# GpSimd multiplies by gamma ahead of the next power, and the tests of the group slots are written another way

## The reference

```python
h_nr  = gelu(x @ w1_nr  + b1_nr)  @ w2_nr  + b2_nr      # condition 0 ("NR")
h_tsr = gelu(x @ w1_tsr + b1_tsr) @ w2_tsr + b2_tsr     # condition 1 ("TSR")
h     = gelu(x @ w1_sr  + b1_sr)                        # condition 2 ("SR"), 512 wide
h_sr  = gelu(h @ w2_sr  + b2_sr)  @ w3_sr  + b3_sr
y = x + (the one that the condition picks, or zeros)
out = (y - mean(y)) * rsqrt(var(y) + 1e-5) * gamma + beta
```

## Time and profile before

| | us |
|---|---|
| median of 3 runs | 112.78 |
| the runs | 111.09, 112.78, 112.89 |
| the profiled execution | 111.2 |
| its span | 109.5 |
| busy: PE, DVE, POOL, ACT | 86.0, 77.6, 68.3, 64.3 |
| first product of the first group | 14.5 |
| TensorE's last instruction ends | 94.7 |
| last scatter issued | 104.87 |

### The profile page before, as it was taken

One profiled execution on the slowest core, in us unless ns is written; L12 is line 12 of the kernel. 1 busy time (PEld: TensorE's weight loads), 2 busy tenths in 40 slices (PEclk: granted clock), 3 DMA queues, 4 the chain that ended last, 5 costly groups with the idle time before them and its releaser, 6 DMA issues.

```text
span 109.5 us, 1829 instructions
## 1 busy us (share of the span) xinstructions
PE 86.0 (79%) x503; PEld 74.9 (68%) x503; DVE 77.6 (71%) x193; ACT 64.3 (59%) x104; POOL 68.3 (62%) x78
## 2 busy tenths in 40 slices
PE   0269969999999999999999999999999976600000
PEld 0157568868889888798998989989899866500000
DVE  5579084762555572839989899899998889699800
ACT  0575229995986045895977959779595870330000
POOL 6427910019777630000796988979879798999850
PEclk9999999999999999999999999999999999995555
DMA  0794788100498991000000404022040130103153
GB/s 2 264 311 142 234 258 298 34 0 3 94 343 205 419 407 73 0 6 0 0 6 22 175 3 174 6 87 105 6 192 6 73 130 6 54 0 154 40 216 144
DMA packets 5459, 12.84 MB, mean 117 GB/s; under 512 B 688, under 2 KB 2752, under 8 KB 5440
## 3 DMA queue, kind: packets, MB, share of 16 engines
q0 software_dynamic: 2880, 9.96, 25.5%
q1 hardware_dynamic: 2540, 2.63, 7.3%
q10 hardware_dynamic: 20, 0.01, 0.0%
HBM read 8.40 MB, written 4.72 MB: 120 GB/s over the span
## 4 chain that ended last, share of the span: by engine, by line
PE 67%; POOL 13%; DVE 4%; DMA 4%; issue 4%; POOLq 2%; ACT 1%; ACTq 1%
PE ps_a L732 8%; PE ps_a L734 8%; PE ps_a L733 7%; PE ps_x L713 7%; PE ps_f L786 6%; PE ps_f L788 6%; PE ps_f L787 6%; POOL xs L346 4%; POOL xs L341 4%; PE ps_f L814 4%; DMA bias_rows<-L_cond_b_sr_dram 4%; PE ps_f L777 3%; POOL rstd L331 3%; PE ps_b L807 2%; PE ps_b L808 2%
## 5 line engine op out<-in xcount | busy, mean ns | idle before, releaser
L331 POOL TENSOR_TENSOR rstd<-hvar,half 128x4 f32<-128x4 f32 x9 | 9.4, 1040 | 15.6 <-DVE hvar L598 15.5
L788 PE MATMUL ps_f<-wf_hi,f_hi 128*128 x64 | 17.9, 280 | 0.0
L786 PE MATMUL ps_f<-wf_hi,f_lo 128*128 x64 | 17.9, 280 | 0.0
L787 PE MATMUL ps_f<-wf_lo,f_hi 128*128 x64 | 17.9, 280 | 0.0
L732 PE MATMUL ps_a<-x_hi,w_lo 128*128 128x512 f32 x40 | 16.5, 413 | 1.1 <-DVE x_lo L643 1.1
L409 ACT ACTIVATE f_hi<-ps_a,bias_cols 128x512 fp32r<-128x512 f32 x16 | 11.0, 688 | 9.6 <-PE ps_a L808 4.7
L734 PE MATMUL ps_a<-x_hi,w_hi 128*128 128x512 f32 x40 | 15.7, 393 | 0.0
L733 PE MATMUL ps_a<-x_lo,w_hi 128*128 128x512 f32 x40 | 15.6, 390 | 0.0
L299 POOL DMA_INDIRECT xs<-x_dram,load_idx x11 | 11.1, 1012 | 6.5 <-DVE load_idx L538 3.6
L413 ACT ACTIVATE xs<-xs,shift,rstd 128x256 f32<-128x256 f32 x23 | 12.1, 593 | 4.3 <-POOL shift L335 4.3
L346 POOL TENSOR_TENSOR xs<-xs,beta_b 128x768 f32<-128x768 f32 (+1 forms) x8 | 14.1, 1762 | 0.5
(11 more groups left out here) (124 smaller groups left out, 191.3 us busy)
## 6 DMA issues: line engine op xcount, KB each, us to landing
w_raw<-L_cond_w_sr_dram SPq DMA_DIRECT2D x2, 512.0 KB, 4.6
wf_raw<-L_cond_w_sr_dram SPq DMA_DIRECT2D x1, 256.0 KB, 5.3
w_raw<-L_cond_w_tsr_dram SPq DMA_DIRECT2D x1, 256.0 KB, 6.5
w_raw<-L_cond_w_nr_dram SPq DMA_DIRECT2D x1, 256.0 KB, 6.8
wf_raw<-L_cond_w_tsr_dram SPq DMA_DIRECT2D x1, 256.0 KB, 6.9
wf_raw<-L_cond_w_nr_dram SPq DMA_DIRECT2D x1, 256.0 KB, 7.1
xs<-x_dram,load_idx POOLq DMA_INDIRECT x11, 6.5
out_dram<-xs,store_idx POOLq DMA_INDIRECT x9, 3.4
```

Source lines behind the costliest of these rows:

```text
L331: nc.gpsimd.tensor_tensor(rstd[:, g, :], hvar[:, g, :], half[:, :], ALU.pow).then_inc(rstd_step, 1)
L786: nc.tensor.matmul(dst, fl[:, kt, toks], w_hi, start=False, stop=False)
L787: nc.tensor.matmul(dst, fh[:, kt, toks], w_lo, start=False, stop=False)
L788: mm = nc.tensor.matmul(dst, fh[:, kt, toks], w_hi, start=False, stop=last)
```

## The change

On GpSimd, times_gamma of group g-1 moves from behind root and shifted of g to in front of them (function pool_group); beta and scatter stay behind. In all engines but SyncE, each_step takes the place of the loops with by_place: the first eight slots are not tested, from slot 8 on an empty slot leads to the finish of the group before it, whose instructions stand directly behind the step that ran. As each route's branch now holds the whole step, TensorE's last layer stands in both. SyncE waits for slots 0 to 6 without tests, then for 10, 9, 8 behind tests, then for 7.

The diff, cut to what matters:

```diff
--- before.py
+++ after.py
@@ -210,31 +210,38 @@
             eng.load(regs, cls_tab[0:1, 0:SLOTS])
             return [eng.snap(r, min_val=0, max_val=EMPTY) for r in regs]
 
-        def by_place(eng, cls, g, normal, second, last):
-
-            def end():
-                if g + 1 < MIN_GROUPS:
-                    second(g)
-                elif g + 1 < SLOTS:
-                    with eng.If(cls[g + 1] < EMPTY):
-                        second(g)
+        def each_step(eng, cls, step, finish):
+
+
+            for s in range(SLOTS + 1):
+                if s < MIN_GROUPS:
+                    step(s)
+                elif s < SLOTS:
+                    with eng.If(cls[s] > NR):
+                        if s == MIN_GROUPS:
+                            finish(s - 1)
+                        else:
+                            with eng.If(cls[s - 1] < EMPTY):
+                                finish(s - 1)
+                            with eng.Else():
+                                pass
                     with eng.Else():
-                        last(g)
+                        step(s)
                 else:
-                    last(g)
-
-            if g + 2 < MIN_GROUPS:
-                normal(g)
-            elif g + 2 < SLOTS:
-                with eng.If(cls[g + 2] < EMPTY):
-                    normal(g)
+                    with eng.If(cls[s - 1] < EMPTY):
+                        finish(s - 1)
+                    with eng.Else():
+                        pass
+
+        def if_next(eng, cls, s, part):
+
+            if s + 1 < MIN_GROUPS:
+                part(s + 1)
+            elif s + 1 < SLOTS:
+                with eng.If(cls[s + 1] < EMPTY):
+                    part(s + 1)
                 with eng.Else():
-                    end()
-            else:
-                end()
-
-        def nothing(g):
-            pass
+                    pass
 
         @block.sync
         def _(sp):
@@ -257,11 +264,14 @@
                 sp.dma_start(W_F[i][0], W_F[i][1]).then_inc(w_in[4 + i], 16)
             sp.wait_ge(tab_done, 1)
             cls = load_classes(sp, "sp_cls")
-            for s in range(SLOTS):
+            for s in range(MIN_GROUPS - 1):
+                sp.wait_ge(stored[s], 16)
+            for s in reversed(range(MIN_GROUPS, SLOTS)):
                 with sp.If(cls[s] < EMPTY):
                     sp.wait_ge(stored[s], 16)
                 with sp.Else():
                     pass
+            sp.wait_ge(stored[MIN_GROUPS - 1], 16)
 
         @block.gpsimd
         def _(pool):
@@ -356,26 +366,27 @@
                     in_=xs[g][:, :, :].rearrange("p t h -> p (t h)"), in_offset=None,
                     bounds_check=last_row, oob_is_err=False).then_inc(stored[g], 16)
 
-            def middle(g):
+            def pool_group(g):
+                if g > 0:
+                    times_gamma(g - 1, POOL_TT)
                 root(g)
                 shifted(g)
                 if g > 0:
-                    times_gamma(g - 1, POOL_TT)
                     plus_beta(g - 1, POOL_TT)
                     scatter(g - 1, False)
 
-            def final(g):
+            def pool_step_of(s):
+                if s > 0:
+                    pool_group(s - 1)
+
+            def pool_finish(g):
                 times_gamma(g - 1, 2)
                 root(g)
                 plus_beta(g - 1, 2)
                 scatter(g - 1, False)
                 scatter(g, True)
 
-            for g in range(SLOTS):
-                with pool.If(cls[g] < EMPTY):
-                    by_place(pool, cls, g, middle, middle, final)
-                with pool.Else():
-                    pass
+            each_step(pool, cls, pool_step_of, pool_finish)
 
         @block.scalar
         def _(act):
@@ -438,50 +449,37 @@
...
+            def act_step(s):
+                f = f_hi[s % 2]
                 if s > 0:
-                    next_x(s)
...
+            each_step(act, cls, act_step, lambda g: normed_second(g - 1))
@@ -646,54 +644,41 @@
...
+            def norm_part(s):
+                if s >= 1:
+                    middle(s - 1)
+                if s == 2:
+                    dve.wait_ge(gamma_done, 1)
+                if s >= 2:
+                    gamma_beta_one(s - 2)
...
+            each_step(dve, cls, dve_step_of, final)
@@ -816,27 +791,24 @@
             pe.wait_ge(bias_done, 1)
             pe.wait_ge(tab_done, 1)
             cls = load_classes(pe, "pe_cls")
-            for s in range(SLOTS + 1):
-                if s < SLOTS:
-                    with pe.If(cls[s] < EMPTY):
-                        if s > 0:
-                            pe.wait_ge(x_lo_done, upto_x(s))
-                            next_x(s)
-                        with pe.If(cls[s] < TSR):
-                            long_first(s)
-                        with pe.Else():
-                            with pe.If(cls[s] < NR):
-                                short_first(TSR, s)
-                            with pe.Else():
-                                short_first(NR, s)
+            def pe_step(s):
                 if s > 0:
-                    with pe.If(cls[s - 1] < EMPTY):
-                        by_place(pe, cls, s - 1, to_f, to_f, to_x)
+                    pe.wait_ge(x_lo_done, upto_x(s))
+                    if_next(pe, cls, s, transpose_x)
+                with pe.If(cls[s] < TSR):
+                    long_first(s)
+                    if s > 0:
+                        last_layer(s - 1, ps_f)
+                    long_second(s)
+                with pe.Else():
+                    with pe.If(cls[s] < NR):
+                        short_first(TSR, s)
                     with pe.Else():
-                        pass
-                if s < SLOTS:
-                    with pe.If(cls[s] < TSR):
-                        long_second(s)
+                        short_first(NR, s)
+                    if s > 0:
+                        last_layer(s - 1, ps_f)
+
+            each_step(pe, cls, pe_step, lambda g: last_layer(g, ps_x))
 
 
 # ---- launch: one core; inputs and outputs as the reference has them ----
```

More of the change, by code:

```diff
@@ new lines, in act_step @@
+            def act_step(s):
+                f = f_hi[s % 2]
+                if s > 0:
+                    if_next(act, cls, s, x_high)
+                with act.If(cls[s] < TSR):
+                    bias_at = act.snap(cls[s].with_bounds(max_val=SR) * 4)
+                    banks = (ps_a[0], ps_a[1], ps_b, ps_a[0])
+                    for m in range(HT):
+                        gelu(banks[m][:, 0, :], h_hi[:, m, :], bias_cols[:, bass.ds(bias_at + m, 1)],
+                             HID * s + m + 1, 1)
+                        if s == 0 and m == 0:
+                            x_high(1)
+                    if s == 0:
+                        other_routes()
+                    if s >= 2:
+                        normed(s - 2)
+                    for m, bank in ((0, ps_a[1]), (1, ps_b)):
+                        gelu(bank[:, 0, :], f[:, m, :], bias_cols[:, 14 + m:15 + m], HID * s + HT + m + 1, 1)
+                with act.Else():
+                    if s == 0:
+                        other_routes()
+                    bias_at = act.snap(cls[s].with_bounds(max_val=NR) * 4)
+                    for m in range(2):
+                        gelu(ps_a[m][:, 0, :], f[:, m, :], bias_cols[:, bass.ds(bias_at + m, 1)],
+                             HID * s + SHORT[m], SHORT_STEP[m])
+                        if s == 0 and m == 0:
+                            x_high(1)
+                    if s >= 2:
+                        normed(s - 2)
@@ L647, in _ @@
             cls = load_classes(dve, "dve_cls")
[L649 to L656, removed]
-                if s > 0:
-                    next_x(s)
[L659 to L690, removed]
-                    with dve.Else():
-                        pass
-                if s < SLOTS:
-                    with dve.If(cls[s] < TSR):
-                        for m, bank in ((0, ps_a[1]), (1, ps_b)):
-                            low(bank[:, 0, :], f[:, m, :], f_l[:, m, :], HID * s + HT + m + 1, 1)
@@ new lines, in norm_part, with dve_step_of @@
+            def norm_part(s):
[3 more added lines that the diff above has]
+                    dve.wait_ge(gamma_done, 1)
+                if s >= 2:
+                    gamma_beta_one(s - 2)
+            def dve_step_of(s):
+                f, f_l = f_hi[s % 2], f_lo[s % 2]
+                if s > 0:
+                    if_next(dve, cls, s, x_low)
+                with dve.If(cls[s] < TSR):
+                    banks = (ps_a[0], ps_a[1], ps_b, ps_a[0])
+                    for m in range(HT):
+                        low(banks[m][:, 0, :], h_hi[:, m, :], h_lo[:, m, :], HID * s + m + 1, 1)
+                        if s == 0 and m == 0:
+                            x_low(1)
+                    if s == 0:
+                        w_low(2)
+                        w_low(3)
+                    norm_part(s)
```

(11 more changed lines are left out.)

54 lines of the change are left out of this document (2 added, 52 removed).

## The result

| | before | changed |
|---|---|---|
| median, us | 112.03 (111.09 to 112.89, 4 runs) | 114.14 (113.35 to 114.41, 4 runs) |
| ratio | | 1.0254, 95% interval 1.019 to 1.0318 |
| profiled execution: span | 109.5 | 112.6 |

The forecast was 111.2 us, with a range of 109.3 to 113.0; the measured time lies above it. Of the four executions of before, 112.78 and 112.89 are slow executions, which the ratio leaves out (it takes before as 111.2 us), while the median in the table, and the 112.0 from which the forecast took its 0.8, hold both kinds.

What follows compares the result with a forecast made beforehand. TensorE's step was taken to bound the middle and GpSimd's list the end. The last scatter, at 104.07 against 104.87, was to come 0.8 us earlier: 112.0 less 0.8 gives 111.2 us, range 109.3 to 113.0.

Steps and rivals of the forecast that it cites:

- GpSimd's list, gamma taken alone: GpSimd from power 6 on: one gamma fewer behind power 6, scatter 8 at 103.00, 1.9 us earlier.
- The case without collision: Rival, chance 0.18: diff on VectorE is not held by a gamma; 1.9 us gained, 110.1 us.
- The collision: VectorE's small SBUF operations wait until GpSimd's running operation ends; diff 7 held 1.3 us, gain 0.8 instead of 1.9.
- The loop that outgrows the step: Rival, chance 0.12: GpSimd's loop of 6.87 us exceeds TensorE's step of 6.89 through longer holds; 111.8 to 113.0 us.
- Diff 8 ... beside a scatter and not held: Last group on VectorE: diff at 98.3 runs beside a GpSimd scatter without waiting; a hold of 0.31 us goes.
- 5.48: VectorE's time in us from diff 8 to the end of its last tiles: 5.79 of before less 0.31.
- A scatter starts 0.29 after its last input: GpSimd's last scatter: VectorE's last tiles end at 103.8, so it starts at 104.07, against 104.87 before.
- Code that is not there in time: Rival, chance 0.12: jumps over more code stall TensorE in mid-kernel; one stall makes +0.7 us (112.7), two +2.3 (114.3).
- TensorE's stall before the last group: The 1.54 us stand of TensorE before the last group's layer goes away, but brings nothing.
- VectorE's tests before the last sum: Seven tests before the last group's sum, with 0.83 us idle, become two; counted within the 0.8 us.
- The end: From the start of the last scatter to the end of the span: 4.6 us, as before.
- The base: Time of the kernel before, from which 0.8 us was taken: 112.0 us, the middle of all four runs.

Runs made afterwards that it cites:

- experiment 6: Changed kernel with VectorE's statistics in PSUM (one copy in SBUF) and TensorE's list of before: 109.47 us, ratio 0.9842 to before.
- 12: Changed kernel with statistics in PSUM and without the gathers of the two empty slots 9 and 10: 109.23 us, ratio 0.9801 to before.
- experiment 2: Kernel before with only gamma moved ahead of the power on GpSimd: 112.17 us, ratio 1.008 to before.
- experiment 10: Changed kernel with power 8 back ahead of gamma 7 in the last group's finish on GpSimd: 112.41 us, ratio 1.0118 to before.
- Experiment 8: Changed kernel without the gathers of the two empty slots 9 and 10: 112.63 us, ratio 1.0167 to before.
- 11: Changed kernel with VectorE's code shifted by 70 instructions that are never executed: 113.37 us, ratio 1.0181 to before.
- experiment 7: Kernel before with only the statistics put in PSUM: 112.12 us, ratio 1.0083 to before.
- experiment 9: Changed kernel with statistics in PSUM, TensorE's list of before and gamma back behind the power: 111.42 us, ratio 1.0007 to before.

## Why the prediction was wrong

- **GpSimd's list, gamma taken alone: right.** The case without collision had power 7 at 93.39 and the last scatter at 103.00. Experiments 6 and 12, where nothing is held, have 93.46 and 103.06 or 103.07.
- **The collision: right in kind and, in the middle, in size.** Each diff of groups 2 to 7 ends with a gamma, the most in 7 (1.20; foreseen 1.3). With gamma alone (2) power 7 is at 94.41, foreseen 94.33. The Trainium skill's rule (GPSIMD Engine Reference, Specifications) named the resource, and the trace agrees; that section does not say how long an operation waits, and the traces show it: to the end of the other, within 0.04 us.
- **The loop that outgrows the step: did not happen.** The powers of groups 2 to 7 follow one another by 6.88 to 6.90 us, TensorE's step (6 and 7: 95.86 - 88.98 = 6.88).
- **"Diff 8 ... beside a scatter and not held": this step failed.** Diff itself came as foreseen, beside the scatter and 0.17 long, but m, 0.09 behind it, was held. The place was not misjudged: all six operations take 0.6 us (92.39 to 92.99 in group 7 of before, 98.79 to 99.38 in experiment 10), so from 99.48 they would have been done at 100.1, before gamma 7 began at 100.31. What was wrong is the premise that only a running operation holds: a gamma that hasn't begun does too, if it stands ready behind a scatter. m took 2.05 us, and the term "5.48", from diff 8 to the end of VectorE's last tiles, measured 7.15 (99.48 to 106.63). Taking the hold away (10) gives 1.0254 - 1.0118 = 1.4% back, some 1.5 us.
- **"A scatter starts 0.29 after its last input": too short here.** That holds where the input is GpSimd's own. Scatter 7 starts 0.80 behind VectorE's tile (105.06, row below, to 105.86), as it does in experiment 2 (103.68 to 104.48), and scatter 8 comes 1.35 behind it, 0.3 us later than by the rule:

```profile
104.37 0.69 DVE L603 TENSOR_TENSOR xs<-ps_a,beta_b 128x512 f32<-128x512 f32 x1
104.98 1.65 DVE L629 SCALAR_TENSOR_TENSOR xs<-ps_x,rstd,beta_b 128x256 f32<-128x256 f32 x4
```

- **Code that is not there in time: the rival that I gave 0.12.** It came once, as priced (1.5; measured 1.38). My argument that the middle of before shows no such stall was no evidence, since the middle of before has no such jump. The Trainium skill's rule (Runtime: NRT & Kernel Launch, Instruction fetch mechanics) spoke against the layout, and the trace agrees in one of seven short groups, where the queues were full besides (4.40 us); in the six others the same jump took 0.34 us at most. The sum put this term at nothing and left it to a rival. Experiment 8 gives 1.0254 - 1.0167 = 0.9% back.
- **TensorE's stall before the last group: gone, and worth nothing, as foreseen.** TensorE's last layer starts at 91.46 without a gap; experiment 6 keeps that stall (1.42) and is as fast as 12 but for 0.4%.
- **VectorE's tests before the last sum: right.** The sum at 96.57 follows without idle time (before 0.83), and they are the half without which gamma's move brings nothing.
- **The end: missed.** I took 4.6 us from the last scatter to the end as given. It became 5.4 by a code load of another engine: 0.8 us.
- **The base.** The 0.8 was taken from 112.0. The ratio's own base is 111.2, so like for like the forecast was 110.4, and the change was misjudged by 3.6 us (+2.8 for -0.8). The three losses add up to about as much, 3.7.

Taken away one at a time, the three losses give 1.4 + 0.9 + 0.7 = 3.0% back; from 1.0254 that leaves 0.996, some 0.5 us under before, where the forecast's sum had 0.8. The changed kernel's own ratio is known to 0.6% only, only 10's interval lies clear of it, and 10 and 11 happened to have a smaller stall on TensorE in their profiled executions, so this is a rough closing of the account, not a proof that nothing else is left.

## What to carry to other kernels

When an operation moves on GpSimd, lay its whole new stretch, and the stretch before it in which it stands ready, over every VectorE operation with two SBUF inputs, not over the first only; giving one input a place in PSUM removed the collision for 0.26 us a group. A test whose target is far away can wait for a code load, and where it lies beside bulk transfers the load waits behind them (4.4 us here, 1.7 to 2.4 with two gathers fewer): put the first such jump into a quiet stretch. Where two lists end together, price a change to one of them with the other as the bound: here each half was worth at most 0.7 us, both 2.65.

## What the runs showed of the hardware

- A GpSimd operation on SBUF that stands ready behind a scatter holds a VectorE operation with two SBUF inputs before it begins itself (2.05 us, from 99.57 on, gamma from 100.31). It did not hold the one that started 0.09 earlier, 0.25 behind the scatter's start (0.17 us); what decides between them no run here shows.
- A scatter started 0.80 us behind a VectorE operation that it waited for, and 0.29 behind one of GpSimd's own.
- A load of code beside a scatter's transfer can delay a few packets of it, and with them the landing: 4.2 to 4.3 us instead of 3.5, with the load 1.8 us behind the scatter's start.
- In experiment 7 TensorE stood for 1.86 us before the last group's layer, and then ran at the lower of its two clock levels (granted 0.50, 1.2 GHz; its row in order of time, then the window from 93 to 95):

```profile
91.52 0.49 PE L786 MATMUL ps_x<-bf_parts,ones 128*128 x1 [1.86 <-issue]
```

```profile
93.00:95.00 2.00, 2.00 (x10) 1.90 (x10) 1.56 (x10) 0.00 (x0) 1.73 (x3) 0.50 0.19 66
```

In before it stood there for 1.54 us and kept 1.00, and in experiment 9 for 1.87 us and kept 1.00 as well (91 to 95 us), so the length of the stand alone does not tell. The lower clock cost nothing, as VectorE came later than TensorE's products.
